# Second attention of an eight-layer kernel: value products for two heads at once in quarter batches, a third exponential buffer, one masked output pass

## The chip, the cores and the metric

The kernel runs on one core of one Trainium2 chip. The metric is the device time of one execution in microseconds (us). The compute engines are TensorE (PE, with its weight loads shown apart as PEld), VectorE (DVE), ScalarE (ACT) and GpSimd (POOL); SyncE (SP) issues nearly all DMAs. They meet only through semaphores.

## The reference

The model is four layers of gated cross-attention, each with a feed-forward block. The change lies in the attention of the second layer. With B*N = 1024 queries and 1024 keys, H = 16 heads of 16 numbers each, it computes (cut):

```
q = (x @ Wq + bq).reshape(1, B * N, H, hd)
kv = (cond @ Wkv + bkv).reshape(1, -1, 2, H, hd)
q = _fq_sym(q * scale, axis=-1);  k = _fq_sym(k, axis=-1);  v = _fq_sym(v, axis=2)     # rounded to 8 bits
attn = softmax(einsum('bhqd,bhkd->bhqk', q, k))
attn = _fq_unsigned(attn, axis=-1)            # rounded to 0..255 of the row's largest
out = einsum('bhqk,bhkd->bhqd', attn, v)
return out @ Wp + bp
```

## The kernel before, in words

The attention's core is 128 steps: 8 tiles of 128 queries (`row_tile`) times 16 heads. `core` unrolls the first 32 steps and puts the other 96 into a hardware loop of two passes of 48 (`BODY`); POOL and SP are unrolled throughout. A step n does this:

- PE multiplies 128 queries by 1024 keys (two matmuls of 512 columns, L1082) into one of three pairs of PSUM banks (`score_banks`); it waits until the exponential of step n-3 is done (`p1_ready`).
- DVE scales the 1024 scores in PSUM and takes their row's minimum (L1227, `m1_ready`).
- ACT takes the exponential into `PE1` (two buffers, L1162) with its row sum (`p1_ready`); it waits for POOL's reading of step n-2 (`y1_ready`).
- POOL computes 255 p + 1024 into fp16 (L1188): adding 1024 rounds to a whole number. It writes `Y1`, of which there are four (`Y_SLOTS`).
- The 128x1024 result is turned (keys onto partitions): by a DMA transpose of SP (L1250) for seven heads of eight, by eight PE transposes (L1094) and an ACT copy (L1145) for every eighth (`by_tensor`, `TURN_EVERY`, `TURN_AT`; PE does it five steps later). The turned weights lie in `PT1`, eight slots.
- Eight steps later (`LAG_V`) PE multiplies by the values: 12 matmuls per head of 128 columns, with 32 columns of weights (L1107 to L1109). The stationary operand `V1` holds each head's 16 columns in a 32-wide field padded with zeros, so that an even and an odd head add up in the same 32 partitions of `OUT_BANK`. Every third matmul takes off the 1024 with `V1_pairs` and the constant `m1024`.

Once per tile, DVE inverts the row sums (L1235), POOL repeats them to 256 columns (L1177), PE turns these (L1117), ACT copies them with the values' step into `scale1` (L1152), and DVE multiplies the 128x256 outputs by it into `xT` (L1221, `o1_ready`). After the core PE projects `xT` (L457).

Before and at the start of the core, DVE quantises the queries in four pairs of tiles (`quantise_queries`, helper `largest1`); the last pair (`LATE_PAIR`) is done between steps 3 and 4 (`LATE_AT`), ACT repeats it at step 8, and SP turns it in front of head 10's transpose. The matmul helper `keep_clock` issues matmuls whose result nobody reads.

After the core SP loads `w3n` as soon as all value products are done (`v1_done`); DVE sums its magnitudes (L1238) before it adds the projection to `X` (L464).

## Time and profile before

| | |
|---|---|
| median of 3 runs | 876.94 us (873.41 to 878.43) |
| profiled execution, its own time | 876.02 us |
| its span | 874.3 us |
| mean granted clock of PE | 0.972 of full |
| busy: PE, DVE, ACT, POOL | 93%, 66%, 44%, 43% of the span |
| first and last score pass of DVE (L1227) | 291.8 and 477.8 us |

The span runs from the first to the last instruction of the profiled execution; its own time has 1.7 us more around it. Times in the rows below are from the span's start. A PE that is shown busy is not at its peak, since matmuls overlap and each is shown with its full latency: for PE the distance between starts says more.

### The profile page before, as it was taken

What the parts mean: (1) busy time and instruction counts of PE and PEld (TensorE: products, weight loads), DVE (VectorE), ACT (ScalarE), POOL (GpSimd) and SP (SyncE); (2) the same over time, 40 slices, a digit from 0 to 9 for tenths busy, and PEclk for the clock granted to TensorE, in tenths of its full rate; (3) what the DMA queues carried; (4) which work ended last, traced back from release to release, by engine and by line L of the source; (5) the groups of instructions that cost most, each with busy time, mean ns of one, the idle gap of its engine ahead of it and who ended that gap; (6) DMA issues with size and microseconds to landing.
All of it is one profiled execution on the core that took longest, in us unless ns stands there. A gap on an engine that the chain in (4) does not pass through costs nothing.

```text
span 874.3 us, 15363 instructions
## 1 busy us (share of the span) xinstructions
PE 809.0 (93%) x5518; PEld 503.8 (58%) x5518; DVE 573.3 (66%) x1212; ACT 387.0 (44%) x668; POOL 373.9 (43%) x392
## 2 busy tenths in 40 slices
PE   7999999999999699999999979879999999999883
PEld 4647776544357256666666635445558967777531
DVE  4958876369664989999998597876621135124955
ACT  3244442311102689989999253646202343331211
POOL 3413403135153367777777261201170027971335
PEclk9999999999999799999999999989999999897998
DMA  9500001102510699999888300540853142991013
GB/s 288 113 0 2 1 1 47 45 0 46 112 36 1 115 172 165 160 154 168 164 161 151 76 1 1 124 132 2 194 165 118 49 139 61 258 247 34 16 13 36
DMA packets 217246, 82.33 MB, mean 94 GB/s; under 512 B 179506, under 2 KB 214990, under 8 KB 217182
## 3 DMA queue, kind: packets, MB, share of 16 engines
q1 hardware_dynamic: 214238, 76.23, 41.1%
q0 software_dynamic: 2944, 5.25, 2.6%
q8 instruction: 39, 0.64, 0.3%
q14 instruction: 25, 0.20, 0.1%
HBM read 33.21 MB, written 8.40 MB: 48 GB/s over the span
## 4 chain that ended last, share of the span: by engine, by line
PE 67%; DVE 10%; issue 7%; DMA 5%; POOL 5%; ACT 4%; SPq 2%; DVEq 0%; POOLq 0%; ACTq 0%
PE psum L1082 6%; PE psum L477 5%; PE psum L653 3%; DMA hT<-hT 3%; PE psum L1664 3%; PE psum L1107 3%; PE psum L633 3%; PE psum L516 3%; PE psum L1332 2%; PE psum L481 2%; PE psum L1109 2%; PE psum L1108 2%; DVE cx L2292 2%; PE psum L1942 2%; PE psum L457 2%
## 5 line engine op out<-in xcount | busy, mean ns | idle before, releaser
L1227 DVE TENSOR_SCALAR_CACHE_REDUCE psum<-psum,arena 128x1024 f32<-128x1024 f32 x128 | 164.6, 1289 | 14.5 <-PE psum L1082 14.0
L1188 POOL TENSOR_SCALAR hT<-arena 128x1024 f16<-128x1024 f32 x128 | 134.0, 1047 | 59.7 <-ACT arena L1162 41.9
L1162 ACT ACTIVATE arena<-psum,am 128x1024 f32<-128x1024 f32 x128 | 142.5, 1116 | 19.6 <-POOL hT L1188 10.6
L334 POOL TENSOR_TENSOR rstd<-ve,neg_half 128x1 f32<-128x1 f32 x64 | 39.5, 621 | 193.4 <-DVE ve L324 192.6
L1107 PE MATMUL psum<-hT,vaug 128*32 128x128 f16 x512 | 93.8, 222 | 2.8 <-DVE xT L1221 1.3
L1108 PE MATMUL psum<-m,arena 128*32 128x128 f16 x512 | 92.6, 220 | 0.0
L1109 PE MATMUL psum<-hT,vaug 128*32 128x128 f16 x512 | 92.5, 220 | 0.0
L1082 PE MATMUL psum<-arena 128*128 128x512 bf16 x256 | 78.8, 391 | 10.4 <-ACT arena L1162 9.1
L1107 PEld LDWEIGHTS psum<-hT,vaug 128*32 128x32 f16 x512 | 49.2, 96 | 50.3 <-issue 46.7
L711 POOL TENSOR_TENSOR arena<-arena,mask 128x1024 f32<-128x1024 f32 x16 | 30.0, 1900 | 56.3 <-PE psum L633 56.3
L1109 PEld LDWEIGHTS psum<-hT,vaug 128*32 128x32 f16 x512 | 49.8, 97 | 0.0
L393 ACT ACTIVATE xT<-psum 128x512 f32<-128x512 f32 x28 | 15.5, 597 | 77.0 <-PE psum L361 76.8
L1108 PEld LDWEIGHTS psum<-m,arena 128*32 128x32 f16 x512 | 49.6, 97 | 0.0
L477 PE MATMUL psum<-xT,arena 128*128 128x512 f32 (+1 forms) x96 | 45.3, 593 | 0.0
L1802 POOL DMA_INDIRECT arena<-moe_out,route x16 | 16.0, 1000 | 60.0 <-DMA moe_out<-arena 56.1
L1578 ACT ACTIVATE arena<-psum 128x1024 f32<-128x1024 f32 x32 | 31.0, 1021 | 23.1 <-PE psum L1535 23.1
L493 ACT ACTIVATE sg<-psum 128x512 f32<-128x512 f32 (+2 forms) x18 | 10.7, 596 | 65.8 <-PE psum L481 51.1
L2006 POOL TENSOR_TENSOR hT<-hT,weights 128x512 f16<-128x512 f32 x32 | 39.3, 1270 | 0.8 <-DMA hT<-in_L_ffn_expert_masks 0.8
L693 ACT ACTIVATE arena<-arena 128x512 f32<-128x512 f32 x32 | 20.2, 630 | 40.7 <-DVE arena L750 40.7
L328 DVE TENSOR_SCALAR xn<-X,mv,rstd 128x256 f32<-128x256 f32 x64 | 34.1, 532 | 2.4 <-POOL rstd L334 1.6
L633 PE MATMUL psum<-arena 128*128 128x512 f32 x64 | 34.8, 630 | 0.8 <-ACT arena L674 0.8
L653 PEld LDWEIGHTS psum<-vaug,arena 128*128 128x128 f32 x256 | 30.9, 191 | 6.3 <-issue 3.9
(405 smaller groups left out, 1755.0 us busy)
## 6 DMA issues: line engine op xcount, KB each, us to landing
hT<-in_L_ffn_expert_masks SPq DMA_DIRECT2D x32, 256.0 KB, 3.7
arena<-in_L_ffn_w_gate SPq DMA_DIRECT2D x2, 1408.0 KB
arena<-in_L_ffn_w_up SPq DMA_DIRECT2D x2, 1408.0 KB
arena<-in_L_ffn_w_down SPq DMA_DIRECT2D x2, 1408.0 KB
moe_in<-xT SPq DMA_DIRECT2D x2, 1024.0 KB, 7.1
hT<-moe_in SPq DMA_DIRECT2D x4, 512.0 KB, 5.9
moe_out<-arena SPq DMA_DIRECT2D x16, 128.0 KB, 1.7
hT<-hT SPq DMA_TRANSPOSE x112, 3.3
```

The lines of the kernel that those rows point to most:

```text
L334: pool.tensor_tensor(rstd[:, t:t + 1], ve[:, t:t + 1], neg_half[:, t:t + 1], ALU.pow).then_inc(sig("ln_rstd"), 1)
L477: mm = pe.matmul(bank[0:fn, :], w[:, c, f0:f0 + fn], xT[:, c, g * HALF:(g + 1) * HALF], start=(c == 0), stop=(c == DC - 1 and lora is None))
L633: ids["s0", n] = ring_v.fill(pe.matmul(bank, qT0[:, i // 2, b * S:(b + 1) * S], kBD0[:, b % 2, i // 2, 4 * (i % 2):4 * (i % 2) + 4, :].rea ...
L653: mm = pe.matmul(bank[:, j * HA:(j + 1) * HA], PT0[:, m % 4, j * S:(j + 1) * S], vaug[:, b, 4 * i + j, :], start=True, stop=True)
L1082: mm = pe.matmul(psum[:, score_banks(c), :][:, g, :], QT[:, bass.ds(row_tile(j, c), 1), pair, :].rearrange("p t q -> p (t q)"), KT[c % 2][ ...
L1107: pe.matmul(o, V1[:, k, c % H, :], PT1[:, c % PT_SLOTS, k, :], start=(first and k == 0), stop=False)
L1108: pe.matmul(o, V1_pairs[:, k // 2, c % H, :], m1024, start=False, stop=False)
L1109: mm = pe.matmul(o, V1[:, k + 1, c % H, :], PT1[:, c % PT_SLOTS, k + 1, :], start=False, stop=(last and k == NB - 2))
L1162: act.activation(PE1[:, c % 2, :], psum[:, score_banks(c), :].rearrange("p a b -> p (a b)"), ACT.Exp, scale=-1.0, bias=am[:, bass.ds(n, 1) ...
L1188: pool.tensor_scalar(Y1[:, n % Y_SLOTS, :], PE1[:, n % 2, :], 255.0, 1024.0, ALU.mult, ALU.add)\
L1227: dve.tensor_scalar(s, s, size1[:, bass.ds(n, 1)], None, ALU.mult, ALU.min, accum_out=am[:, bass.ds(n, 1)])\
L2006: pool.tensor_tensor(wm[:, ep % WM_PAIRS, :, k, :, :], mk[:, e % 6, :, :].rearrange("p o (c n) -> p c o n", c=DC), w3n3.rearrange("p o (c ...
```

## The change

In the core, PE no longer does a head's value products in one batch per step. It gathers four heads (`GROUP`), and does their 24 matmuls in quarters over the next four steps (in halves over two steps for the last group of a tile). A matmul now takes the values of two neighbouring heads as 32 stationary columns and the turned weights of both heads as 256 moving columns; of the 32x256 result only the diagonal blocks are wanted. Within a quarter the matmuls alternate between two pairs of heads, whose outputs lie in different groups of 32 partitions. `V1` and `V1_pairs` lose their zero padding. DVE's pass over the outputs reads 128x512 instead of 128x256 and writes `out_parts`; POOL then multiplies its two halves by the parity masks `par` and adds them into `xT` (`add_parts`). The exponentials get a third buffer (`sg`), the turned weights four more slots (in `xn`). `V1_pairs` is made by DVE instead of POOL, and POOL's zeroing of `V1` goes. The late pair of queries is quantised in four portions behind steps 3 to 6, and turned in front of head 20's transpose. In steps 0 to 10 PE gets two `keep_clock` matmuls of 512 columns after the scores. That every eighth head is turned by TensorE stays as it was.

```diff
-        V1_pairs = a.tile([NB // 2, H, 2 * HD], FP16)
-        size1 = a.tile([P])
-        scale1, inv_wide = a.tile([DC, P]), a.tile([D])
-        V1 = Arena(vaug.rearrange("p t h d -> p (t h d)")).tile([NB, H, 2 * HD], FP16)
+        V1, V1_pairs = a.tile([NB, D], FP16), a.tile([NB // 2, D], FP16)
+        size1, inv_wide = a.tile([P]), a.tile([D])
...
-        PT_SLOTS, Y_SLOTS = 8, 4
+        PT_SLOTS, Y_SLOTS = 12, 4
+        out_parts = qf.rearrange("p t d -> p (t d)")[:, 0:2 * DC * P].rearrange("p (c i q) -> p c i q", i=2, c=DC)
+        scale1 = qf[:, 2, :].rearrange("p (c q) -> p c q", c=DC)
...
-        TURN_EVERY, LAG_TURN, LAG_V = 8, 5, 8
-        TURN_AT, LAG_INVERT, LAG_REPEAT, LAG_SPREAD, LAG_OUT = 3, 3, 2, 6, 9
+        GROUP, TURN_EVERY, TURN_AT, LAG_TURN, LAG_V = 4, 8, 3, 5, 8
+        LAG_INVERT, LAG_REPEAT, LAG_SPREAD, LAG_OUT, LAG_ADD = 3, 2, 6, LAG_V + 2, LAG_V + 1
         LATE_PAIR = NB // 2 - 1
-        LATE_AT = {"round": 3, "repeat": 8, "turn": 10}
+        LATE_AT = {"round": 3, "repeat": 8, "turn": 20}
...
+        def pe1(c):
+
+            return PE1[:, c % 3, :] if c % 3 < 2 else sg.rearrange("p a b -> p (a b)")
...
+            def values(c0, k0, k1):
+                for k in range(k0, k1, 2):
+                    for which in range(3):
+                        for c in range(c0, c0 + GROUP, 2):
+                            chunk, rows = c % H // 8, slice(16 * (c % 8), 16 * (c % 8) + 32)
+                            part = slice(c % H * HD, c % H * HD + 32)
+                            o = psum[rows, OUT_BANK, chunk * 2 * P:(chunk + 1) * 2 * P]
+                            if which == 1:
+                                pe.matmul(o, V1_pairs[:, k // 2, part], bc(m1024.unsqueeze(1), [P, 2, P]), start=False, stop=False)
+                                continue
+                            at = k + which // 2
+                            mm = pe.matmul(o, V1[:, at, part], pt1(c, 2)[:, :, at, :], start=(at == 0), stop=(at == NB - 1))
+                            if at == NB - 1:
+                                mm.then_inc(sig("v1_done"), 1)
...
+                    if isinstance(j, int) and c < LAG_V + GROUP - 1:
+                        keep_clock(pe, psum[:, OUT_BANK, :], 2)
...
-                    for k in range(0, NB, 2):
-                        pe.matmul(o, V1[:, k, c % H, :], PT1[:, c % PT_SLOTS, k, :], start=(first and k == 0), stop=False)
-                        pe.matmul(o, V1_pairs[:, k // 2, c % H, :], m1024, start=False, stop=False)
-                        mm = pe.matmul(o, V1[:, k + 1, c % H, :], PT1[:, c % PT_SLOTS, k + 1, :],
-                                       start=False, stop=(last and k == NB - 2))
-                    mm.then_inc(sig("v1_done"), 1)
+                    if c % H == GROUP - 1:
+                        wait_step(pe, "o1_read", row_tile(j, c) + -1)
+                    for i in range(GROUP):
+                        wait_turned(pe, j, c - i)
+                for i in range(GROUP):
+                    m, c = trails(j, c0, LAG_V + i)
+                    if m is not None and c % GROUP == GROUP - 1:
+                        parts = 2 if c % H == H - 1 else GROUP
+                        if i < parts:
+                            values(c - GROUP + 1, i * NB // parts, (i + 1) * NB // parts)
...
-                wait_step(act, "y1_ready", n + -2)
-                act.activation(PE1[:, c % 2, :], psum[:, score_banks(c), :].rearrange("p a b -> p (a b)"), ACT.Exp,
+                wait_step(act, "y1_ready", n + -3)
+                act.activation(pe1(c), psum[:, score_banks(c), :].rearrange("p a b -> p (a b)"), ACT.Exp,
...
-            pool.wait_ge(ring_v.evacuated, ids["v1"])
-            pool.tensor_tensor(V1_pairs, V1[:, 0::2, :, :], V1[:, 1::2, :, :], ALU.add).then_inc(sig("v1_pairs_ready"), 1)
+            def add_parts(t):
+
+                pool.wait_ge(sig("o1_read"), t + 1)
+                for i in range(2):
+                    pool.tensor_scalar(out_parts[:, :, i, :], out_parts[:, :, i, :], par[:, i:i + 1], None, ALU.mult)\
+                        .then_inc(sig("o1_masked"), 1)
+                pool.wait_ge(sig("o1_masked"), 2 * (t + 1))
+                pool.tensor_tensor(xT[:, :, t * P:(t + 1) * P], out_parts[:, :, 0, :], out_parts[:, :, 1, :], ALU.add)\
+                    .then_inc(sig("o1_ready"), 1)
...
+            dve.tensor_tensor(V1_pairs, V1[:, 0::2, :], V1[:, 1::2, :], ALU.add).then_inc(sig("v1_pairs_ready"), 1)
...
-                    dve.tensor_tensor(xT[:, :, bass.ds(t * P, P)], psum[:, OUT_BANK, 0:DC * P].rearrange("p (c q) -> p c q", c=DC),
-                                      scale1, ALU.mult).then_inc(sig("o1_ready"), 1)
+                    wait_step(dve, "o1_ready", t + -1)
+                    read = dve.tensor_tensor(out_parts, psum[:, OUT_BANK, :].rearrange("p (c i q) -> p c i q", c=DC, i=2),
+                                             bc(scale1.unsqueeze(2), [P, DC, 2, P]), ALU.mult)
+                    read.then_inc(sig("o1_read"), 1)
...
-                if isinstance(j, int) and n == LATE_AT["round"]:
-                    quantise_queries(LATE_PAIR)
+                if isinstance(j, int) and n is not None and LATE_AT["round"] <= n < LATE_AT["round"] + 4:
+                    next(late, None)
...
-                wait_step(sp, "v1_done", n - PT_SLOTS)
-                sp.dma_start_transpose(PT1[:, n % PT_SLOTS, :, :], Y1[:, n % Y_SLOTS, :]).then_inc(turned(n % H), 16)
+                if n >= PT_SLOTS:
+                    wait_values(sp, 0, n - PT_SLOTS)
+                sp.dma_start_transpose(pt1(n, 1).rearrange("p s k q -> p (s k) q"), Y1[:, n % Y_SLOTS, :]).then_inc(turned(n), 16)
```

## Rows read from the trace of the kernel before

**Rows 1.** One line's instructions: DVE's score pass (L1227), its first and last start.
```profile
L1227 DVE TENSOR_SCALAR_CACHE_REDUCE psum<-psum,arena x128: 1237/1292/1294, 291.8 to 477.8; 128x1024 f32<-128x1024 f32 x128
```

**Rows 2.** Timeline of DVE: score pass of step 32 (start us, us, engine line ...).
```profile
341.94 1.29 DVE L1227 TENSOR_SCALAR_CACHE_REDUCE psum<-psum,arena 128x1024 f32<-128x1024 f32 x1 [0.15 <-issue]
```

**Rows 3.** Timeline of all engines: one step in the loop, and a turn by PE.
```profile
403.69 0.61 PE L1082 MATMUL psum<-arena 128*128 128x512 bf16 x2
...
404.22 0.23 PE L1107 MATMUL psum<-hT,vaug 128*32 128x128 f16 x1
...
404.48 1.29 DVE L1227 TENSOR_SCALAR_CACHE_REDUCE psum<-psum,arena 128x1024 f32<-128x1024 f32 x1
...
404.85 0.22 PE L1109 MATMUL psum<-hT,vaug 128*32 128x128 f16 x1
...
405.00 0.61 PE L1082 MATMUL psum<-arena 128*128 128x512 bf16 x2
...
410.69 0.61 PE L1094 MATMUL psum<-identh,hT 128*128 128x128 f16 x8
```

**Rows 4.** Timeline of PE: column-tiled matmuls in the third attention, and full-width ones.
```profile
262.82 2.95 PE L516 MATMUL psum<-arena,hT 128*128 128x256 f32 x12
...
583.74 0.61 PE L1554 MATMUL psum<-arena 128*32 128x256 f32 x8
584.17 0.61 PE L1550 MATMUL psum<-arena 128*32 128x256 f32 x8
```

**Rows 5.** Timeline of DVE: quantising of queries, score passes back to back, an output pass.
```profile
289.93 0.69 DVE L1001 TENSOR_TENSOR arena<-arena,qr 128x512 f32<-128x512 f32 x1
...
296.63 0.68 DVE L995 TENSOR_REDUCE am<-arena 128x32 f32<-128x512 f32 x1
...
298.47 1.21 DVE L1001 TENSOR_TENSOR arena<-arena,qr 128x512 f32<-128x512 f32 x1
...
300.06 1.28 DVE L1227 TENSOR_SCALAR_CACHE_REDUCE psum<-psum,arena 128x1024 f32<-128x1024 f32 x1
...
301.27 1.28 DVE L1227 TENSOR_SCALAR_CACHE_REDUCE psum<-psum,arena 128x1024 f32<-128x1024 f32 x1
...
330.60 0.42 DVE L1221 TENSOR_TENSOR xT<-psum,arena 128x256 f32<-128x256 f32 x1
```

**Rows 6.** Timeline of ACT: the copy of a turned head, and the next exponential.
```profile
389.62 1.01 ACT L1145 ACTIVATE hT<-psum 128x1024 f16<-128x1024 f16 x1
390.53 1.12 ACT L1162 ACTIVATE arena<-psum,am 128x1024 f32<-128x1024 f32 x1
```

**Rows 7.** Timeline of POOL: repeating the inverses, then two rounding passes; a wait.
```profile
320.56 2.17 POOL L1188 TENSOR_SCALAR hT<-arena 128x1024 f16<-128x1024 f32 x2 [3.70 <-DMA hT<-hT]
...
394.31 0.40 POOL L1177 COPY arena<-qr 128x256 f32<-128x256 f32 x1
394.79 2.17 POOL L1188 TENSOR_SCALAR hT<-arena 128x1024 f16<-128x1024 f32 x2
```

**Rows 8.** Groups of instructions by form, POOL: a 128x256 product (busy us, mean ns).
```profile
L2324 POOL TENSOR_TENSOR cx<-cx,weights 128x256 f32<-128x256 f32 x8 | 5.9, 742 | 16.7 <-ACT cx L2179 16.6
```

**Rows 9.** Windows (busy by engine; PEclk, DMA share, GB/s last).
```profile
300.00:310.00 10.00, 7.08 (x53) 4.07 (x54) 8.62 (x14) 8.46 (x13) 4.36 (x5) 0.65 0.74 112
340.00:470.00 130.00, 128.06 (x1389) 80.41 (x1388) 120.96 (x195) 119.33 (x206) 97.72 (x98) 1.00 0.93 162
420.00:442.00 22.00, 21.79 (x240) 13.76 (x238) 21.14 (x34) 20.58 (x35) 16.91 (x17) 1.00 0.85 162
```

**Rows 10.** SP's transposes (L1250) of the whole core: issue to landing.
```profile
DMA to landing us min/median/max: 3.1/3.3/5.3
```

**Rows 11.** Timeline: DVE before the core and behind it.
```profile
283.00 0.69 DVE L995 TENSOR_REDUCE am<-arena 128x32 f32<-128x512 f32 x1 [2.43 <-ACT arena L1137]
...
486.68 0.42 DVE L1221 TENSOR_TENSOR xT<-psum,arena 128x256 f32<-128x256 f32 x1 [5.94 <-PE psum L1109]
...
490.82 1.62 DVE L1238 TENSOR_REDUCE gam<-arena 128x1 f32<-128x1408 f32 x1 [3.71 <-DMA arena<-in_L_ffn_w]
```

More of the change, by code:

```diff
@@ L933, in turned, with turn_pe, wait_values, pt1 @@
         def turned(h):
-            return sig(f"pt1_slot{h % PT_SLOTS}_landed")
+            return sig(f"y1_slot{h % Y_SLOTS}_landed")
         def by_tensor(c):
             return c % TURN_EVERY == TURN_AT
+        def turn_pe(j, c):
+            return j * (BODY // TURN_EVERY) + c // TURN_EVERY
         def wait_turned(eng, j, c):
-            each = 1 if by_tensor(c) else 16
-            eng.wait_ge(turned(c), j * (each * BODY // PT_SLOTS) + each * (c // PT_SLOTS + 1))
-        def wait_turn_pe(eng, j, c):
-            eng.wait_ge(sig("y1_turned"), j * (BODY // TURN_EVERY) + c // TURN_EVERY + 1)
+            if by_tensor(c):
+                wait_step(eng, "y1_copied", turn_pe(j, c))
+                return
+            slot = range(c % Y_SLOTS, NS, Y_SLOTS)
+            before, each = (sum(not by_tensor(h) for h in slot if h <= last) for last in (c, BODY - 1))
+            eng.wait_ge(turned(c), j * (16 * each) + 16 * before)
+        def wait_turn_pe(eng, j, c):
+            wait_step(eng, "y1_turned", turn_pe(j, c))
+        def wait_values(eng, j, c):
+            eng.wait_ge(sig("v1_done"), j * (2 * BODY // GROUP) + 2 * (c // GROUP + 1))
+        def pt1(c, heads):
+            s = c % PT_SLOTS
+            return PT1[:, s:s + heads, :, :] if s < 8 else PT1_late[:, s - 8:s - 8 + heads, :, :]
+        def pe1(c):
+            return PE1[:, c % 3, :] if c % 3 < 2 else sg.rearrange("p a b -> p (a b)")
         def score_banks(c):
@@ L993, in largest1, with largest1_steps @@
         def largest1(dve, step, v, scaled, large, size, inv):
+            for _ in largest1_steps(dve, step, v, scaled, large, size, inv):
+                pass
+        def largest1_steps(dve, step, v, scaled, large, size, inv):
             step(dve.tensor_reduce(large, v, AX.X, ALU.max, apply_absolute_value=True))
+            yield
             step.wait()
@@ L999, in largest1 @@
             step(dve.reciprocal(inv, size))
+            yield
             step.wait()
             step(dve.tensor_tensor(scaled, v, bc(inv.unsqueeze(2), v.shape), ALU.mult))
+            yield
             step.wait()
@@ L1090, in step @@
                     wait_step(pe, "y1_ready", m)
[L1091 to L1092 removed]
+                    wait_step(pe, "y1_copied", turn_pe(j, c) + -1)
+                    wait_step(pe, "scale1_ready", row_tile(j, c) + -1)
                     for k in range(NB):
@@ L1187, in xa1_pool, with quantise_steps @@
                     wait_turned(pool, 0, n - Y_SLOTS)
-                pool.tensor_scalar(Y1[:, n % Y_SLOTS, :], PE1[:, n % 2, :], 255.0, 1024.0, ALU.mult, ALU.add)\
+                pool.tensor_scalar(Y1[:, n % Y_SLOTS, :], pe1(n), 255.0, 1024.0, ALU.mult, ALU.add)\
                     .then_inc(sig("y1_ready"), 1)
-                t, h = divmod(n - LAG_REPEAT, H)
-                if t >= 0 and h == H - 1:
-                    repeat_inverse(t)
+                for lag, work in ((LAG_REPEAT, repeat_inverse), (LAG_ADD, add_parts)):
+                    t, h = divmod(n - lag, H)
+                    if t >= 0 and h == H - 1:
+                        work(t)
             repeat_inverse(NB - 1)
+            add_parts(NB - 1)
         def xa1_dve(dve, step):
             def quantise_queries(p):
+                steps = quantise_steps(p)
+                for _ in steps:
+                    pass
+            def quantise_steps(p):
                 dve.wait_ge(ring_a.evacuated, ids["q1", 2 * p + 1])
```

48 lines of the change are left out of this document (20 added, 28 removed).

## The prediction

> **What bounds the kernel now.** I first read the instructions of one line, DVE's score pass, because it runs exactly once per step. From its first to its last start the core takes 186.0 us for 127 steps [rows 1]. Step 32, the first of the hardware loop, starts at 341.94 [rows 2]. So the ramp of 32 steps takes 50.1 us, and the 95 steps behind it take 135.9 us: 1.43 us a step, 22.9 us a tile of 16.
>
> Then the timeline of one step [rows 3]. PE's scores start at 403.69, the first value product at 404.22, the last at 404.85, the next scores at 405.00. PE's cycle is 1.31 us without a gap that anybody else makes: 12 value products 0.057 apart (0.68) and 0.63 for two score matmuls with the changes to and from the narrow form. DVE's pass starts at 404.48, 0.18 after the scores' end at 404.30. DVE looks busy for 1.29, yet it follows PE. A turn by PE is 8 matmuls in 0.61, some 0.45 of PE's time when they are pipelined like the others. A tile costs PE at least 16 x 1.31 + 2 x 0.45 = 21.9 us, and the tile takes 22.9: PE binds, and the real pace is 4.5% above its sum.
>
> **The value products.** Before, 12 x 128 columns a head; now 24 x 256 columns for four heads, which is 1536 columns a head as before. Fewer instructions by themselves give nothing: 256 columns at 0.057 per 128 are 0.114, six of them 0.68. What can give something is that neighbours now write different groups of 32 partitions. The core before never does that (a head's 12 all write the same group), so the nearest rows are the third attention's, whose 32-wide matmuls go round four groups: eight of them, 256 columns f32, start in 0.43, or 0.054 each. Full-width matmuls of 256 columns f32 take 2.95 for twelve, 0.246 each [rows 4]. Four groups thus run four to one. For two groups I take two to one: 0.34 a step. The ends are 0.68 (no overlap) and 0.32 (0.054 each). PE's step becomes 0.63 + 0.34 = 0.97, its tile 16 x 0.97 + 0.9 = 16.4 us. PE stops being the bound.
>
> **What is late next.** For each other engine I sum a tile.
> - DVE: two passes whose input is ready start 1.21 apart (300.06, 301.27), not 1.29. The output pass was 0.42 for 256 columns; for 512 I take the 512-column product, 0.69, which is 0.27 more [rows 5]. With 0.2 for the reciprocal: 16 x 1.21 + 0.69 + 0.2 = 20.3 us.
> - ACT: an exponential 1.12, a turned head's copy 0.91 until the next may start [rows 6]. 16 x 1.12 + 2 x 0.91 = 19.7, and the two small copies for the scales, an estimated 0.3 each by their eighth of the columns and a start-up: 20.3 us. Not changed.
> - POOL: a rounding pass is half of 2.17, the repeat 0.48 [rows 7]. New per tile: two masks of 128x256, by the 128x256 copy 0.40 each, and a sum, by the nearest product 0.74 [rows 8]. 16 x 1.085 + 0.48 + 1.54 = 19.4 us; it was 17.8. At the cheap end the additions cost 1.2, at the dear one 2.2 (three times 0.74): 19.1 to 20.1.
> - DMA: 14 transposes of 262,144 bytes. At 162 GB/s the engines' share was 0.85 in one stretch and 0.93 over the long one [rows 9], so full load is 191 or 174 GB/s: 1.38 or 1.50 us each, 19.3 or 21.1 us a tile. I take the first, since throughput in the two stretches was equal and only the time packets stood in line differed.
>
> So four resources stand between 19.3 and 20.3. The third exponential buffer and the twelve slots are what lets them run close to that; alone, at PE's old pace, they would be worth nothing. I put the same 4.5% on 20.3 that lay on PE's sum: 21.2 us a tile, 1.325 a step. The bound below is 20.3 (1.27).
>
> **The sum.** Steps 32 to 127: 95 x (1.43 - 1.325) = 10.0 us off. Ramp: before, value products began at step 8; the same 0.105 for the 24 steps behind gives 2.5 off. The quantising of the late pair took 3.43 us in one piece (296.63 to 300.06) [rows 5]; in four portions the same instructions stay on DVE, a near-bound engine, so I take nothing for the split. Ends: 2 us gained, because ACT and POOL no longer drain, and 2 lost. Its product of 128x512 took 1.21 beside a running POOL pass and 0.69 in the pass before, without one [rows 5]. The Trainium skill, "SBUF — State Buffer", section "Who interferes with whom", says that DVE and GpSimd share a port pair as an exclusive lock, taken by a DVE product with two SBUF inputs against a GpSimd read. By that rule each of some three portions now meets a POOL pass of its own, on average half a pass more each, and the sum would be about 0.7 us worse.
>
> SP: the two query transposes move from in front of head 10 to in front of head 20; queued behind them are the Y transposes from 20 on, for these POOL, for POOL in turn ACT. Once before, POOL stood 3.70 us for a DMA at 320.56 [rows 7]; I take the same stall at its new place. `keep_clock`: 22 matmuls, about 0.46 a step in steps without value products, so a PE step of 1.1 beside DVE's 1.21: nothing. With a half clock it would be 2.2 for those steps, but the clock there was 0.65 before [rows 9], so it can as well pay: from -1 to +3 us. POOL's and PE's added waits name work that is done earlier: `o1_read` comes right behind DVE's pass; a Y slot is free when landing comes 3.3 us after issue [rows 10] with the POOL pass 1.1 and two signals, 4.6 of 5.3 us for four steps. `V1_pairs` on DVE stands ahead of 283.00, where DVE had idled 2.43 us for ACT; twice the 512-column product, 1.4, fits.
>
> Tail: when the last head has landed, 24 matmuls in two groups (1.37) follow where 12 (0.68) did: 0.7 late for the `w3n` load. DVE's pass and POOL's 1.54 come on top for the projection, but DVE adds nothing before it has summed `w3n`, which ended at 492.44, 5.3 us behind the old output pass [rows 11]; PE needs one projected tile ready by then. They cost 0; without that cover 1.8.
>
> Sum on the profiled execution: 876.0 - 10.0 - 2.5 + 0.7 = 864.2 us. The runs' median is 0.9 higher than that execution: **865 us**, with 857 to 870 as this case's own range. Low end: 1.27 a step (119 x 0.055 = 6.5 less) and 2 from the ramp.
>
> **The rivals.**
> 1. *The turned weights set the pace.* Four Y slots chain POOL to the DMA: landing was 3.3 in the middle but 5.3 at most [rows 10], and 5.3 + 1.3 over four steps is 1.65. Heavier load lengthens the lines; for it speaks the share of 0.93, against it that 162 GB/s went through at 0.85. At 1.39 a step: 119 x 0.04 = 4.8 off, 0.7 on: 873 us, right at the mark of 0.5%. The same mark holds if POOL's additions meet locks.
> 2. *The column groups don't overlap*, so the change doesn't do its main thing. Then PE's step is 0.63 + 0.68 = 1.31, as before. Tail: 24 x 0.114 = 2.7 instead of 0.68. 877 to 879 us. Against it: rows 4.
> 3. *PE's clock falls* because PE now idles a third of each step; this one ends slower. The granted clock was 1.00 over the long stretch where PE never stood, and 0.65 behind the quantising gap, where it did [rows 9]. At 1.2 instead of 2.4 GHz a step costs 0.46 more for the scores, 0.34 for the values, 0.06 for turns: 1.83, or 0.5 over the new pace. The gain of 11.8 is gone and 4.4 more lost once 32 of the 128 steps run so; with 48 of them it is 889 us. Against it: the gaps are some 0.35 us each, not microseconds.
>
> **How the numbers follow.** This kernel's measurement can tell about 0.5% (4.4 us) from no change. My forecast has 0.60, rival 1 0.20, rival 2 0.12, rival 3 0.06, 0.02 for the rest. Faster by over 0.5% (below 872.5): the forecast and half of rival 1, 0.70. Within: 0.22, the rest of rival 1 and most of rival 2. Slower: 0.08. The range that holds 8 in 10 goes from the floor of the sums, 857, to rival 2's edge, 877.
>
> **What would show it.** Right: score passes 1.3 to 1.35 apart; value products of a quarter starting in pairs, six in about 0.35; PE waiting for ACT's exponential before the scores (it hardly did); DVE's output pass near 0.69; POOL additions near 1.5 a tile; `w3n`'s sum at about 479. Wrong: six products spread over 0.68 (rival 2); POOL waiting for DMA in most groups of four, landing above 4 (rival 1); a granted clock under 0.95 in the loop (rival 3); DVE spacing in the loop above 1.21 even where PE is early, which would lift DVE's floor: at 1.29 it is 21.5 a tile, and the gain shrinks by half.

## The result, and the profile after

The changed kernel took 879.79 us (median, 870.03 to 886.57), the one before 875.36 (865.24 to 879.63) on the same chips: a ratio of 1.0071, with a 95% interval of 1.0036 to 1.0106. I had forecast 865 us in a range of 857 to 877. The kernel is slower, and the prediction is wrong.

DVE's score pass of the changed kernel is L1289 (engine op xcount, duration min/median/max, first and last start):

```profile
L1289 DVE TENSOR_SCALAR_CACHE_REDUCE psum<-psum,arena x128: 1202/1290/1295, 290.3 to 479.0; 128x1024 f32<-128x1024 f32 x128
```

From first to last start the core takes 188.6 us, where it took 186.0 [rows 1]; my terms made it 173.5. The span goes from 874.3 to 877.9: 1.5 less ahead of the core (290.3 for 291.8), 2.6 more in it, 7.0 more from its last score pass to the first product of the next feed-forward (38.0 us, from 479.0 to 517.0, for 31.0), and 4.6 less behind that. The last term is not put down to the change: that stretch, with the same work, took 358 to 367 us in the fifteen profiled runs below, whatever was changed ahead of it. The core and the stretch behind it are what is to be explained.

The window of [rows 9] again, then the first 10 us behind the last output pass:

```profile
340.00:470.00 130.00, 105.97 (x846) 42.55 (x845) 115.95 (x190) 115.96 (x202) 109.00 (x112) 0.92 0.88 158
...
490.00:500.00 10.00, 6.41 (x19) 3.67 (x14) 4.19 (x8) 0.00 (x0) 2.67 (x4) 0.50 0.22 72
```

PE was busy for 128 of 130 us and is now busy for 106, at less than the full clock. DVE and ACT, which I expected to become the busiest, do 3 to 5 us less in this window than before. POOL does 11 more. Its groups (busy us, mean ns | idle before, releaser):

```profile
L1240 POOL TENSOR_SCALAR hT<-arena 128x1024 f16<-128x1024 f32 x60 | 62.8, 1047 | 14.1 <-ACT arena L1206 7.3 <-DMA hT<-hT 1.9 <-DMA xn<-hT 1.5
L1240 POOL TENSOR_SCALAR hT<-sg 128x1024 f16<-128x1024 f32 x31 | 32.5, 1047 | 5.8 <-ACT sg L1206 3.1 <-DMA hT<-hT 0.8
L1228 POOL TENSOR_SCALAR arena<-arena,par 128x256 f32<-128x256 f32 x10 | 9.2, 925 | 0.5
L1231 POOL TENSOR_TENSOR xT<-arena 128x256 f32<-128x256 f32 x5 | 3.6, 726 | 0.4
```

A mask takes 0.925 us. I had taken 0.40, from a copy of the same size. The rounding above it does four times as many numbers in 1.05. With the sum (L1231) a tile's outputs hold POOL for 2.65 us in one piece, not 1.54. What follows such a piece, in the timeline of all engines:

```profile
427.09 1.83 POOL L1228 TENSOR_SCALAR arena<-arena,par 128x256 f32<-128x256 f32 x2
...
429.01 0.73 POOL L1231 TENSOR_TENSOR xT<-arena 128x256 f32<-128x256 f32 x1
...
429.83 1.05 POOL L1240 TENSOR_SCALAR hT<-sg 128x1024 f16<-128x1024 f32 x1
430.25 1.03 PE L1126 MATMUL psum<-arena 128*128 128x512 bf16 x2
...
431.06 1.11 ACT L1206 ACTIVATE sg<-psum,am 128x1024 f32<-128x1024 f32 x1 [1.51 <-POOL hT L1240]
...
432.32 0.61 PE L1126 MATMUL psum<-arena 128*128 128x512 bf16 x2 [0.58 <-ACT sg L1206]
```

ACT fills its three places, then stands 1.51 us for POOL to empty one. It does so once in each tile of this window, at the same step, for 1.3 to 1.9 us. PE's next scores wait for ACT in turn, and DVE for PE. Two matmuls of scores take 1.03 in place of 0.61: the clock is at its lower level there. The whole chain is in the waits of the same window (in total, times, longest us); DVE's 13.4 us were 8.7 before:

```profile
PE psum L1126 <- ACT arena L1206: 16.4, 26, 2.0
...
DVE psum L1289 <- PE psum L1126: 13.4, 18, 2.1
...
ACT arena L1206 <- POOL hT L1240: 7.3, 5, 1.9
...
ACT sg L1206 <- POOL hT L1240: 3.0, 2, 1.5
```

The column groups (32 stationary columns, whose outputs lie in one group of 32 partitions) do overlap: the products of two pairs of heads start together, the next two 0.11 later, six of them in 0.33.

```profile
434.54 0.29 PE L1114 MATMUL psum<-hT,arena 128*32 128x256 f16 x2
434.66 0.28 PE L1111 MATMUL psum<-m,arena 128*32 128x256 f16 x2
434.77 0.28 PE L1114 MATMUL psum<-hT,arena 128*32 128x256 f16 x2
```

Behind the core ([rows 11] for before):

```profile
488.49 0.29 PE L1114 MATMUL psum<-hT,arena 128*32 128x256 f16 x2 [3.33 <-DMA hT<-hT]
...
490.54 0.69 DVE L1282 TENSOR_TENSOR arena<-psum,arena 128x512 f32<-128x512 f32 x1 [8.59 <-PE psum L1114]
491.33 1.83 POOL L1228 TENSOR_SCALAR arena<-arena,par 128x256 f32<-128x256 f32 x2 [7.38 <-DVE arena L1282]
493.25 0.72 POOL L1231 TENSOR_TENSOR xT<-arena 128x256 f32<-128x256 f32 x1
...
494.07 2.05 PE L458 MATMUL psum<-weights,xT 128*128 128x256 f32 x4 [3.59 <-issue]
...
496.48 0.48 DVE L465 SCALAR_TENSOR_TENSOR X<-psum,gates,X 128x256 f32<-128x256 f32 x1
```

The first addition to X comes 17.5 us behind the last score pass, where it was 14.6, and the feed-forward's first product 20.5 behind that, where it was 16.4 (508.8 - 492.4). PE had stood 3.33 us for a transfer, and then 3.59 more before the projection; a projected tile then takes 2.05 to 2.08 for 1.13, for the first four tiles.

### The profile page after: what moved, and what is told of

It is laid out like the page before. It is cut to its first block, busy times and chain, and to the rows that moved or that the text cites. A ratio compares the mean times of both kernels' runs of the same rounds, so it can differ in the third digit from the quotient of the medians.

```text
span 877.9 us, 13962 instructions
## 1 busy us (share of the span) xinstructions
PE 782.5 (89%) x4772; PEld 450.9 (51%) x4772; DVE 568.8 (65%) x1213; ACT 385.1 (44%) x668; POOL 387.9 (44%) x414
## 4 chain that ended last, share of the span: by engine, by line
PE 63%; DVE 10%; POOL 7%; issue 6%; DMA 6%; ACT 5%; DVEq 0%; POOLq 0%; ACTq 0%; SPq 0%
PE psum L478 6%; POOL hT L1240 4%; PE psum L654 3%; PE psum L1726 3%; PE psum L634 3%; PE psum L458 3%; DMA hT<-hT 3%; PE psum L517 3%; PE psum L1395 2%; PE psum L482 2%; PE psum L1126 2%; DVE cx L2354 2%; DMA xn<-hT 2%; PE psum L1970 2%; PE psum L362 2%
## 5 line engine op out<-in xcount | busy, mean ns | idle before, releaser
L1289 DVE TENSOR_SCALAR_CACHE_REDUCE psum<-psum,arena 128x1024 f32<-128x1024 f32 x128 | 158.8, 1286 | 22.2 <-PE psum L1126 21.4
L1240 POOL TENSOR_SCALAR hT<-arena 128x1024 f16<-128x1024 f32 x86 | 90.0, 1047 | 38.7 <-ACT arena L1206 27.7
L1206 ACT ACTIVATE arena<-psum,am 128x1024 f32<-128x1024 f32 x86 | 96.0, 1120 | 19.1 <-POOL hT L1240 12.2
L1126 PEld LDWEIGHTS psum<-arena 128*128 (+1 forms) x256 | 15.5, 98 | 78.2 <-ACT arena L1206 37.2
L1206 ACT ACTIVATE sg<-psum,am 128x1024 f32<-128x1024 f32 x42 | 47.0, 1120 | 5.0 <-POOL hT L1240 3.0
L1240 POOL TENSOR_SCALAR hT<-sg 128x1024 f16<-128x1024 f32 x42 | 44.0, 1047 | 10.5 <-ACT sg L1206 6.5
L1114 PE MATMUL psum<-hT,arena 128*32 128x256 f16 x352 | 43.9, 287 | 5.1 <-DMA hT<-hT 3.3
L1640 ACT ACTIVATE arena<-psum 128x1024 f32<-128x1024 f32 x32 | 31.0, 1021 | 20.7 <-PE psum L1597 20.7
L346 PE MATMUL psum<-identh 128*128 128x512 f16 (+1 forms) x132 | 37.3, 391 | 2.7 <-issue 2.3
L1111 PE MATMUL psum<-m,arena 128*32 128x256 f16 x256 | 37.4, 289 | 0.0
L1114 PEld LDWEIGHTS psum<-hT,arena 128*32 128x32 f16 x352 | 17.9, 98 | 35.1 <-issue 27.2
```

Of the source, the lines that this page charges most:

```text
L346: pe.matmul(unread.rearrange("p (a n) -> p a n", n=n), identh, bc(identh[:, 0:n].unsqueeze(1), [P, columns // n, n]), start=True, stop=True)
L1111: pe.matmul(o, V1_pairs[:, k // 2, part], bc(m1024.unsqueeze(1), [P, 2, P]), start=False, stop=False)
L1114: mm = pe.matmul(o, V1[:, at, part], pt1(c, 2)[:, :, at, :], start=(at == 0), stop=(at == NB - 1))
L1126: mm = pe.matmul(psum[:, score_banks(c), :][:, g, :], QT[:, bass.ds(row_tile(j, c), 1), pair, :].rearrange("p t q -> p (t q)"), KT[c % 2][ ...
L1206: act.activation(pe1(c), psum[:, score_banks(c), :].rearrange("p a b -> p (a b)"), ACT.Exp, scale=-1.0, bias=am[:, bass.ds(n, 1)], accum_o ...
L1240: pool.tensor_scalar(Y1[:, n % Y_SLOTS, :], pe1(n), 255.0, 1024.0, ALU.mult, ALU.add)\
```

## The experiments

The core is always counted from the first to the last start of DVE's score pass, the tail from there to the feed-forward's first product. The last column is the ratio of the runs, 12 for most experiments (6 for e1 and e2, 8 for e7) and 20 for the changed kernel. Core and tail are of one profiled run each: between the changed kernel and its control, which differ by a few register instructions far behind, they are 0.2 and 1.7 us apart, so a difference of a microsecond or two in the tail alone shows little.

| kernel | POOL for a tile's outputs | core | tail | ratio to before (95%) |
|---|---|---|---|---|
| before | none | 186.0 | 31.0 | 1 |
| changed | 2.65 in one piece | 188.6 | 38.0 | 1.0071 (1.0036 to 1.0106) |
| c0_control | the same | 188.4 | 36.3 | 1.0053 (1.0020 to 1.0086) |
| e1_no_masks | 0.73 | 175.1 | 34.4 | 0.9891 (0.9841 to 0.9941) |
| e2_no_pool_outputs | none | 176.5 | 33.7 | 0.9893 (0.9854 to 0.9931) |
| e5_same_group_order | 2.65 | 188.5 | 36.6 | 1.0041 (1.0007 to 1.0076) |
| e3_spread_masks | 2.65 in three pieces | 181.2 | 39.2 | 1.0000 (0.9971 to 1.0030) |
| e4_tail_clock | 2.65 | 188.0 | 33.5 | 1.0020 (0.9986 to 1.0055) |
| e6_padded | none | 175.3 | 34.1 | 0.9902 (0.9865 to 0.9938) |
| e7_padded_clock | none | 174.4 | 32.8 | 0.9905 (0.9861 to 0.9948) |
| e8_padded_same_group | none | 180.8 | 32.8 | 0.9946 (0.9909 to 0.9983) |
| e9_padded_two_places | none | 182.8 | 33.3 | 0.9974 (0.9932 to 1.0016) |
| e10_before_third_place | none | 183.9 | 30.7 | 0.9944 (0.9906 to 0.9982) |
| e11_padded_idle_masks | 1.85 | 181.6 | 35.6 | 0.9998 (0.9961 to 1.0035) |
| e13_masks_two_ops | 1.69 | 181.1 | 36.7 | 0.9996 (0.9948 to 1.0044) |
| e14_two_ops_spread | 1.69 in three pieces | 178.5 | 36.4 | 0.9940 (0.9891 to 0.9989) |

**Is it POOL's block?** First the changed kernel with the bounded waits that all share, then without masks, without any of POOL's work on outputs, and with the value products' order turned.

> The changed kernel itself, with one addition that all kernels of this study carry: the waits on the sorted tiles' finishing counts, in the third feed-forward's combination, are taken against the larger of the loaded count and 1. That is some register instructions on an engine that waits there anyway. Every theory: 0.998 to 1.002 of the changed kernel, so about 1.007 of the kernel before, core of 128 heads 188 to 189 us from the first score pass to the last.

```diff
-act.wait_ge(ring_v.evacuated, act.snap(regs[i], min_val=1, ...))
+act.wait_ge(ring_v.evacuated, smax(act.snap(regs[i], min_val=-1, ...), 1))
```

> The two mask products of a tile on POOL are left out (so the other head's product stays in each output, and the result is not the reference's); POOL's sum of the two parts stays. Theory 1 (POOL's block of two masks at 0.92 us and a sum at 0.73, 2.65 us in one piece, makes ScalarE wait for the round's buffer, TensorE wait for ScalarE, and the clock fall in the gap): POOL's block is 0.75, its tile 16 x 1.12 + 0.48 + 0.75 = 19.1 us; the core falls from 188.6 to 176 to 181 us, the kernel to 0.985 to 0.992 of the one before, and the granted clock of the core rises over 0.9. Theory 2 (the pace is set by the turned weights, in order, 12 slots and batches of four heads): the core stays within 1.5 us of 188.6, the kernel at 1.004 to 1.007. Theory 3 (TensorE's pairs draw the clock down by themselves): core within 3 us, clock where it was.

```diff
-                for i in range(2):
-                    pool.tensor_scalar(out_parts[:, :, i, :], out_parts[:, :, i, :], par[:, i:i + 1], None, ALU.mult)...
-                pool.wait_ge(sig("o1_masked"), 2 * (t + 1))
```

> POOL does nothing for the outputs: VectorE's output pass takes 256 columns of one parity (every odd head's output is left out, so the result is not the reference's) straight to its place. Theory 1: POOL's tile is 16 x 1.12 + 0.48 = 18.4 us, VectorE's pass 0.42 in place of 0.69; another 1 to 2 us off the core against the kernel without masks, and the stretch from the last score pass to the feed-forward's first product falls from 38 to about 33 us: 0.978 to 0.986 of the kernel before. Theory 2: core within 1.5 us of 188.6, only the tail gives 3 to 4 us back: 1.000 to 1.003. Theory 3: as theory 2, with a low clock in the core.

```diff
-read = dve.tensor_tensor(out_parts, psum[:, OUT_BANK, :].rearrange(...), bc(scale1.unsqueeze(2), [P, DC, 2, P]), ALU.mult)
+read = dve.tensor_tensor(xT[:, :, bass.ds(t * P, P)], psum[:, OUT_BANK, :].rearrange(...)[:, :, 0, :], scale1, ALU.mult)
-                    work(t)      # add_parts
```

> The same value products with the pair of heads as the outermost loop, so that products next to each other write the same 32 columns of the array and can't run beside each other. Theory 1 (the overlap works, and POOL's block is what binds): six products take 0.63 in place of 0.33 us, TensorE's tile rises by 16 x 0.3 = 4.8 us to 21.2, which with the stalls behind POOL's block is above the changed kernel's 23.6: core 190 to 196 us, kernel 1.010 to 1.05 of the one before. If instead TensorE had that much slack in each tile, core and kernel stay within 0.2% of the changed kernel, and the whole first part of the change was worth nothing.

```diff
-for k in range(k0, k1, 2):
-    for which in range(3):
-        for c in range(c0, c0 + GROUP, 2):
+for c in range(c0, c0 + GROUP, 2):
+    for k in range(k0, k1, 2):
+        for which in range(3):
```

The control repeats the changed kernel. Without the two masks the core falls by 13.3 us. Its window:

```profile
340.00:470.00 130.00, 105.20 (x896) 42.55 (x894) 123.03 (x203) 125.53 (x217) 109.05 (x110) 0.99 0.98 173
```

ACT is busy for 125.5 of 130, the clock is back, and DVE's wait for PE is down from 13.3 in the control to 4.5. A tile takes 21.1 us from step 64 on (21.5 from step 32), against my 21.2. So theory 1 stands, even above its numbers (it allowed 176 to 181), and theory 2 falls: twelve slots, batches of four and the transfers stayed, and the DMA share rose to 0.98. Taking the sum away too brings no more (176.5), where theory 1 had 1 to 2 us more.

The run e5 was meant to take the overlap away. Its trace shows that it did not:

```profile
403.75 0.29 PE L1115 MATMUL psum<-hT,arena 128*32 128x256 f16 x2
403.87 0.28 PE L1112 MATMUL psum<-m,arena 128*32 128x256 f16 x2
403.98 0.28 PE L1115 MATMUL psum<-hT,arena 128*32 128x256 f16 x2
```

The program now has three products of one column group and then three of the other, and still they start two by two, 0.01 apart; from first start to last a quarter's six take 0.24 us, for 0.23 in the control. Only in the half batches, where six of one group come in a row, is it more: 0.79 for 0.56. That makes about 0.5 us of PE's time a tile, not the 4.8 of the expectation. So the unchanged 188.5 us do not say what the overlap is worth while POOL binds; no run here does. What e5 adds is on the clock: granted 0.96 in the window, 0.94 in the control and 0.92 in the changed kernel, at the same core. That speaks against the clock as a cause of its own.

**Piece or sum, and the tail.**

> The same three POOL instructions for a tile's outputs, but one each behind the roundings of steps LAG_ADD, LAG_ADD + 2 and LAG_ADD + 4, in place of all three in a row. POOL's work per tile stays 21.2 us, its longest piece between two roundings falls from 2.65 to 0.93 us. Theory 1a (the stall is the block: it exceeds what three exponentials can hide): most of the gain of the kernel without masks comes, core from 188.4 to 176 to 180 us, kernel 0.990 to 0.998 of the one before. Theory 1b (POOL's sum per tile binds, 21.2 us plus what its queue loses, so spreading can't help): core 183 to 188 us, kernel 0.998 to 1.005.

```diff
-for lag, work in ((LAG_REPEAT, repeat_inverse), (LAG_ADD, add_parts)):
+for lag, work in ((LAG_REPEAT, repeat_inverse), (LAG_ADD, mask_part(0)), (LAG_ADD + 2, mask_part(1)), (LAG_ADD + 4, add_parts)):
```

> The changed kernel with 15 unread 512-column products before the wait for the last four heads' turned weights and 16 before the wait for the last output, so that TensorE does not stand still there. Theory A (the tail's 7 us come mostly from the clock that falls to half in the 3.3 us gap, so that the last products, the spreading and the first four tiles of the projection take twice as long): granted clock of the 10 us behind the last scores over 0.85, a projection tile 1.13 in place of 2.1 to 2.3 us, kernel 3 to 5 us shorter than the control, 1.000 to 1.003 of the one before. Theory B (the tail is set by POOL's masks and sum, 2.65 us, and by the transfers): at most 1.5 us.

```diff
+                if isinstance(j, int) and m == NS - 1:
+                    pe.wait_ge(sig("p1_ready"), NS)
+                    keep_clock(pe, psum[:, 0, :], 15)
...
             pe.wait_ge(sig("p1_ready"), NS)
+            keep_clock(pe, psum[:, 0, :], 16)
             pe.wait_ge(sig("o1_ready"), NB)
```

Both 1a and 1b are half right. The same POOL work in three pieces gives 7.2 of the 13.3 us back (181.2, at the edge of 1a's range, inside 1b's for the ratio), so the rest, 6.1, is put down to POOL's time in sum. That is argued: the pieces of 0.93 are not e1's single one of 0.73 either.

In the tail, e4 keeps PE's clock at 1.00 (a projected tile 1.13 from the first on) and shortens the stretch by 2.8 us against the control, 4.5 against the changed kernel: from the first addition to the feed-forward 16.7 us, which is before's 16.4. The same addition still comes 16.8 behind the last score pass for 14.6 before. That part is not POOL's: it is 17.2 in the control, 17.7 in e1, where POOL does 0.73, and 17.2 in e2, where it does nothing for the outputs. It comes with the last value product, which starts 8.7 us behind the last score pass in the kernel before, 11.1 in the changed one and 10.8 in the control. POOL's masks show behind the first addition: 19.2 us there in the control, 16.7 in e1 and 16.4 in e2. The ratio is 0.33% under the control's, with intervals that overlap, so in the whole kernel's time this is not shown.

**The same order of work without POOL.**

> The changed kernel's order of work (batches of four heads in quarters, alternating column groups, 12 slots, third place for exponentials, each eighth head turned by TensorE) on the value layout of the kernel before: 32 columns a head of which 16 are zeros, 12 products of 128 columns a head in place of 12 of 256 for two. The other head's product does not arise, VectorE's output pass takes 256 columns and writes the outputs itself, POOL does nothing for them; the complete computation. TensorE streams as many columns. Theory 1 (POOL's block was the whole loss of the core): core 174 to 177 us as without masks, kernel 0.982 to 0.990 of the one before. Rival (twice the number of value products at 128 columns does not overlap as well, or their weight loads bind: 0.057 us each in the kernel before against 0.11 for a pair of 256): TensorE's step back to 1.31 us, core 180 to 186 us, 0.992 to 1.000.

```diff
-V1, V1_pairs = a.tile([NB, D], FP16), a.tile([NB // 2, D], FP16)
+V1 = Arena(...).tile([NB, H, 2 * HD], FP16)        # 32 columns a head, 16 of them zero
...
-                        for c in range(c0, c0 + GROUP, 2):
+                        for c in (c0, c0 + 2, c0 + 1, c0 + 3):
+                            chunk, rows = c % H // 8, slice(32 * (c % 8 // 2), 32 * (c % 8 // 2) + 32)
+                            o = psum[rows, OUT_BANK, chunk * P:(chunk + 1) * P]
...
-read = dve.tensor_tensor(out_parts, ...)
+read = dve.tensor_tensor(xT[:, :, bass.ds(t * P, P)], psum[:, OUT_BANK, 0:DC * P].rearrange(...), scale1, ALU.mult)
```

> The kernel e6_padded with the unread products of e4_tail_clock: if theory A holds there, it comes out 2 to 4 us under e6_padded, 0.978 to 0.987 of the kernel before; if theory B, within 1.5 us of it.

```profile
340.00:470.00 130.00, 106.18 (x1501) 53.64 (x1499) 123.32 (x205) 126.52 (x219) 105.33 (x105) 1.00 0.97 173
```

This one does the complete computation and beats both kernels: 0.9902 of before. PE is busy for the same 106 us with nearly twice the products, and a quarter's twelve start within 0.29 us. So what overlaps is the columns, whether 12 matmuls stream them or 6, and the rival of dearer weight loads falls. ACT, at 126.5 of 130, now sets the pace. Keeping the clock in its tail gives 1.3 us there and nothing in the ratio.

**What each part is worth once POOL is out of the way.**

> The kernel e6_padded with the products of a head in a row, so that neighbours write the same column group. Theory X (without POOL's block VectorE and ScalarE set the pace, 20.3 us of work a tile, and TensorE's 21 us a tile without overlap comes back as the bound, like in the kernel before): core 182 to 187 us in place of 175.3, kernel 0.996 to 1.003 of the one before. Theory Y (the overlap is worth nothing, since the batches alone give TensorE its slack; the same edit on the changed kernel moved nothing): core within 1.5 us of 175.3, kernel within 0.2% of e6_padded.

```diff
-for k ... for which ... for c in (c0, c0 + 2, c0 + 1, c0 + 3):
+for c in (c0, c0 + 1, c0 + 2, c0 + 3): for k ... for which ...
```

> The kernel e6_padded with two places for exponentials in place of three. Theory X (the third place only lets ScalarE run ahead of POOL over its longest piece, now a copy of 0.40 us, so it is worth 0 to 2 us once the masks are gone): 0.989 to 0.993 of the kernel before. Rival (ScalarE needs it for the two copies and the turned head's copy, which come in a cluster): core 178 to 184 us, 0.994 to 1.000.

```diff
-            return PE1[:, c % 3, :] if c % 3 < 2 else sg.rearrange("p a b -> p (a b)")
+            return PE1[:, c % 2, :]
-                wait_step(act, "y1_ready", n + -3)
+                wait_step(act, "y1_ready", n + -2)
```

> The kernel before with the third place for exponentials alone. My prediction took TensorE as its bound, so: within 1 us of it, 0.999 to 1.001, core 186 us. Rival (the kernel before is held by ScalarE waiting for POOL and not by TensorE): core 178 to 183 us, kernel 0.992 to 0.997.

The edit of e10 is that of e9 the other way round, in the kernel before.

> The kernel e6_padded with two mask products a tile on POOL again, 0.92 us each in one piece, on data that nobody reads and without a wait, so that only POOL's time differs and no chain of outputs does. POOL's tile is 18.4 + 1.85 = 20.3 us. Theory P (POOL's time is the cause, by its sum and block): core 178 to 184 us, kernel 0.994 to 0.999 of the one before, ScalarE waiting for POOL behind each block. Theory Q (the cause is the chain pass, masks, sum, next pass, not the time): core within 1.5 us of 175.3, 0.990.

```diff
+def idle_masks(t):
+    for i in range(2):
+        pool.tensor_scalar(parts[:, :, i, :], parts[:, :, i, :], par[:, i:i + 1], None, ALU.mult)
```

In e8 the overlap is cut down, not gone: a quarter's twelve products take 0.42 us from first start to last in place of 0.29, a half batch's 24 take 1.09 in place of 0.63, together some 2.4 us of PE's time a tile. For this part of it the core is 5.5 us longer. Theory X, which took all of the overlap for gone, gave 182 to 187; what the whole is worth stays open.

Without the third place the core is 7.5 us longer. Theory X gave 0 to 2 us and was wrong, the rival was right in size: ACT's waits for POOL go from 0.8 us to 8.2 in the window. They are 29 short ones of at most 0.6 us all over the tile, not the cluster of the rival's reason. Nor was that place worth nothing in the kernel before: e10 is 2.1 us shorter in the core, between its two theories, and 0.56% in the ratio (4.9 us, of which the core shows less than half). PE never waits there (128.7 of 130 us busy), and the tile is still 22.7, not my sum of 21.9.

In e11 nothing waits for the masks and nobody reads them, and yet the core is 6.3 us longer, the kernel 1% slower than e6_padded. So POOL's time costs by itself (theory P). The chain of outputs with the sum alone cost nothing: e1 has it and e2 doesn't.

**Why does a mask take 0.92 us?** The prediction's price was from a copy, so one kernel, run once, has each form once or twice, behind one tile each.

> The kernel e6_padded with two unread POOL instructions behind each tile, of another form for each tile, all over 128x256 single-precision numbers (one over 128x512): a product by a scalar of each partition in place (the mask's form); by a constant in place; by the partition's scalar over an unbroken run; by it into another tile; a copy; a product by the mask broadcast as a second operand; one product over 512; a product and a sum by constants in place. Theory M (it is the per-partition scalar that costs: the rounding, with constants and two operations, takes 1.05 us for 1,024 numbers): the forms with it take 0.9 us, those with constants 0.3 to 0.5, the broadcast one 0.7. Rival N (single-precision results or the in-place access cost, whatever the scalar): all products take 0.8 to 0.95 us, and the copy alone 0.4. Rival O (the broken run of two times 128 costs): the unbroken one takes 0.4.

```diff
+1235  pool.tensor_scalar(one, one, s, None, ALU.mult)                  # the mask
+1237  pool.tensor_scalar(one, one, 1.0, None, ALU.mult)
+1239  pool.tensor_scalar(run, run, s, None, ALU.mult)
+1241  pool.tensor_scalar(other[:, i, :, :], one, s, None, ALU.mult)
+1243  pool.tensor_copy(other[:, i, :, :], one)
+1245  pool.tensor_tensor(one, one, bc(s.unsqueeze(2), [P, DC, P]), ALU.mult)
+1247  pool.tensor_scalar(flat[:, 0:2 * DC * P], flat[:, 0:2 * DC * P], s, None, ALU.mult)
+1249  pool.tensor_scalar(one, one, 1.0, 0.0, ALU.mult, ALU.add)
```

```profile
L1235 POOL TENSOR_SCALAR arena<-arena,par 128x256 f32<-128x256 f32 x2 | 1.8, 930 | 0.1
L1239 POOL TENSOR_SCALAR arena<-arena,par 128x256 f32<-128x256 f32 x2 | 1.8, 924 | 0.1
L1241 POOL TENSOR_SCALAR arena<-arena,par 128x256 f32<-128x256 f32 x2 | 1.8, 922 | 0.1
L1237 POOL TENSOR_SCALAR arena<-arena 128x256 f32<-128x256 f32 x2 | 1.7, 848 | 0.1
L1247 POOL TENSOR_SCALAR arena<-arena,par 128x512 f32<-128x512 f32 x1 | 1.6, 1563 | 0.1
L1245 POOL TENSOR_TENSOR arena<-arena,par 128x256 f32<-128x256 f32 x2 | 1.2, 612 | 0.1
L1249 POOL TENSOR_SCALAR arena<-arena 128x256 f32<-128x256 f32 x2 | 0.8, 404 | 0.1
L1243 POOL COPY arena<-arena 128x256 f32<-128x256 f32 x2 | 0.7, 398 | 0.1
```

None of my three theories holds. Not the partition's scalar (0.85 with a constant), nor the place, nor the broken run (0.92 in all three). A product followed by the addition of 0.0 takes 0.40, the product alone 0.85: the form with one operation is the slow one. (L1249 ran behind the last tile, with the core over; e13 repeats it inside the core.) The trace of the kernel before had it, in two groups of POOL that I didn't look for, between 187 and 195 us:

```profile
L1477 POOL TENSOR_SCALAR small<-hT 128x1024 bf16<-128x1024 f32 x2 | 5.6, 2785 | 0.2
L1475 POOL TENSOR_SCALAR hT<-hT,q 128x1024 f32<-128x1024 f32 x2 | 2.4, 1194 | 31.0 <-DVE q L985 31.0
```

L1477 subtracts a constant and does nothing more: 2.79 us. L1475, as wide, multiplies by a partition's scalar and adds a constant: 1.19. They differ in the type that they write, too. So the changed kernel was run with two operations in its masks.

> The changed kernel with one thing more in its two mask products: a second operation, the addition of 0.0. The result is the same. In the run of forms a product of this kind took 0.40 us with two operations and 0.85 (constant) or 0.92 (the partition's scalar) with one. Theory M2 (the missing second operation is what costs): masks 0.40 to 0.48 each, POOL's block 1.55 to 1.7 us as my prediction had it, POOL's tile 20.0; core 175 to 180 us, kernel 0.988 to 0.996 of the one before. Rival (the partition's scalar costs its 0.9 with two operations too): masks 0.9, core 188, 1.005.

```diff
-pool.tensor_scalar(out_parts[:, :, i, :], out_parts[:, :, i, :], par[:, i:i + 1], None, ALU.mult)
+pool.tensor_scalar(out_parts[:, :, i, :], out_parts[:, :, i, :], par[:, i:i + 1], 0.0, ALU.mult, ALU.add)
```

> The same, with the three POOL instructions behind three different roundings, as in e3_spread_masks. If a block of 1.6 us still costs something over one of 0.73: core 1 to 4 us under e13_masks_two_ops, kernel 0.987 to 0.992. If a third place for exponentials covers such a block whole, as my prediction took: within 1 us of it, apart from the last tile, where the order is the same.

```profile
L1229 POOL TENSOR_SCALAR arena<-arena,par 128x256 f32<-128x256 f32 x12 | 5.7, 483 | 0.6
```

The masks of e13 take 0.483 each, POOL's piece 1.69. The core falls from 188.4 to 181.1 us, a little above the 175 to 180 that theory M2 gave, and spread over three steps (e14) to 178.5: 0.994 of before, where 0.987 to 0.992 was expected, and still 3.4 us over e1. The rival of e13 is out. The ratio of e13, 0.9996, holds only 0.57% of that against the control, with overlapping intervals; and the 0.988 to 0.996 expected was missed. Its profiled run was one of its slower ones (877.1 us, median 871.4), with the longest stretch of all behind the feed-forward's start (366.6 us).

## Why the prediction was wrong, point by point

- **The step that failed: POOL's additions at 1.54 us a tile** ("two masks of 128x256, by the 128x256 copy 0.40 each"), with the dear end at 2.2. They took 2.65. The sum, 0.73, was right. The masks' price was off by a factor of 2.3 because the nearest row that I took was of the same size and not of the same form; the row of the same form, L1477, gives 0.70 for 256 numbers by its quarter alone, and it was not read. It would have given 2.1 for the additions, the dear end of the sum; the whole 2.65 stands in no row of the kernel before. The Trainium skill, "GPSIMD Engine Reference", section "Engine selection", calls one-input work there roughly line-rate and two-input work about twice as slow as on VectorE; by that rule a mask would cost less than the sum. The trace disagrees: 0.925 against 0.73.
- **A reading beside it.** A rounding pass was taken as half of 2.17, the length of two records that overlap. Back to back they start 1.12 apart, so POOL's tile was 0.6 us short before any mask. With 1.12 and 2.65 it is 16 x 1.12 + 0.48 + 2.65 = 21.1 us: the largest of the four sums, over the 20.3 on which the forecast was built.
- **The second failure: that POOL's work counts only by its sum per tile.** I compared 19.4 with 20.3 and let it go. e13 has nearly my price (POOL's tile is 16 x 1.12 + 0.48 + 1.69 = 20.1) and a core of 181.1, not 173.5. A piece that stands between two roundings is taken from what three places can hold ahead; spreading it gives 2.6 us at 1.69 and 7.2 at 2.65. With a single 0.73 left nothing is lost. Of the 7.6 us between e13 and the forecast the one piece is thus 2.6, and e1 alone is 1.6 over the forecast; the 3.4 between e14 and e1 are put down to the masks' remaining 0.97 us a tile.
- **Terms that were right.** Values in 0.34 a step: 0.33. DVE's output pass near 0.69: 0.692. Its passes 1.21 apart when it isn't kept waiting: 1.21 to 1.22. ACT's tile of 20.3: 126.5 of 130 us (e6) is 20.7 per tile of 21.3. The 4.5% on top, carried over from PE's sum with no reason of its own: 21.2 forecast for steps 32 to 127, 21.5 and 21.4 measured where POOL is out of the way (e1, e6; 21.1 and 21.3 from step 64). The ramp's 2.5 us: 2.7 in e1, 0.1 in the changed kernel. The whole core: 173.5 forecast, 175.1 and 175.3 there. So the sum was right within 1% for a kernel that did not have the masks. The 0.7 us that the prediction set beside its sum, for VectorE's split quantising meeting POOL, did not come: one product met a pass as before, 1.28 us for 1.21.
- **Rival 1**, turned weights, transfers or POOL at 1.39 a step, priced with POOL meeting locks as a side remark, was nearest in kind. DMA was not it: in e1 DMA carried 173 GB/s at a share of 0.98, and in the changed kernel a landing took 3.3 us in the middle, as before. **Rival 2** is refuted by the pairs. **Rival 3**: the clock fell to 0.92 in the loop, which I had named as its sign, and not for PE's idling as such: in e6 PE is as idle (106 of 130 us busy) at 1.00. The gaps were other: none over 1.5 us in e6's window, three in the changed kernel's and four in the control's (0.94), and without the masks, in e1, one and 0.99. So the fall goes with POOL's block and adds to it; how much of the core's loss is the clock's own was not separated, except that e5 lost as much at 0.96.
- **"Alone, at PE's old pace, they would be worth nothing"**: the third place alone gave 2.1 us and 0.56% in the kernel before. PE had no wait in those rows, and still its 4.5% above the sum were not all its own; how the place helps there stays open.
- **Tail: +0.7** forecast, +7.0 measured, 2.9 of it up to the first addition to X and 4.1 behind. The first part is the 0.7 of the sum, mis-sized: the last value product starts 11.1 us behind the last score pass for 8.7, since the last batch of 24 waited 3.33 us for a transfer and ended at the lower clock. `w3n`'s load waits for it, and its sum came at 494.88, 15.9 us behind the last score pass, where it was 13.0. DVE's and POOL's parts, costed at nothing under the `w3n` cover, cost nothing up to there (17.2 with and without POOL's work, control and e2). Behind it they did: PE stood 3.59 us for them, and the lower clock for four projected tiles was no term of mine.

My chance of 0.08 for a slower kernel left the whole case to the clock. POOL's block, which is what decided, had no slower branch of its own.

## What to carry to other kernels

Price an instruction by a row of its own form, its number of operations too, before its own size; then ask how long the engine is held in one piece, and how many places the engine ahead of it has, not only whether the engine's sum fits. In the changed kernel what its parts give (a part of the overlap 5.5 us in e8, the third place 7.5 in e9) was hidden: its core was longer than before. So take a suspected block out before judging the rest. And read in the trace whether an experiment's edit did what it was meant to: e5's did not, and its time alone would have told a false story. Where masks cost more than the zeros that they replace, the zeros were cheap: the padded values streamed as many columns.

## What the runs showed of the hardware

- POOL's tensor_scalar over 128x256 single-precision numbers: 0.40 us with product and sum by constants (e12), 0.48 with a partition's scalar and a constant (e13), but 0.85 and 0.92 to 0.93 with the product alone (e12); a product with a broadcast second tensor 0.61, a copy 0.40 (e12).
- Matmuls of 32 columns to two column groups, turn about, start in pairs: 0.33 us for six of 256 columns, and PE's busy time was the same with twelve of 128 (e6).
- They need not take turns: with three of one group and then three of the other they started in pairs all the same (e5, 0.24 us from first start to last for 0.23). With six and six of 128 columns a part of the overlap was lost (e8, 0.42 us for 0.29).
- PE idle for 24 of 130 us in gaps of up to 1.3 us kept a granted clock of 1.00 (e6); idle for as long, with three or four gaps of 1.5 to 2.0 us among them, it was at 0.92 and 0.94 (changed kernel, control).
